# One full 32-bit matmul in place of three split ones, and a state update with high and low keys in one weight block

## What is computed

```python
# feed-forward branch (weights ternary, scales per output)
h = silu(x @ w1.T * s1) * (x @ w2.T * s2);  h = gelu(h @ h1.T * sh1);  h = gelu(h @ h2.T * sh2);  y = h @ w3.T * s3
# attention branch: gated linear attention over chunks of 64 tokens
b = cumsum(gt)                                   # log decay per key
o = (qt * exp(b)) @ S + A @ vt                   # A[i,j] = sum_k q[i,k] k[j,k] exp(b[i,k]-b[j,k]), j <= i
S = exp(btot)[:, None] * S + (kt * exp(btot - b)).T @ vt
o = (o + shift * residual_weight) * silu(gate);  o = o * rms(o) * norm_weight;  y = o @ down_w.T
```

## Time and profile before

| | us |
|---|---|
| median of 3 runs | 1988.01 (1987.57 to 1988.39) |
| span of the profiled execution, first to last instruction | 1984.5 |
| TensorE matmuls busy | 1967.8 (99% of the span) |
| TensorE weight loads busy | 1954.0 (98%) |
| VectorE busy | 1576.1 (79%) |
| ScalarE busy | 1258.2 (63%) |
| GpSimd busy | 68.6 (3%) |

### The profile page before, as it was taken

The page is one execution under the profiler, slowest core; times in us unless marked ns, Lnnn a source line. Parts: engine busy times, 40 slices in busy tenths (PEclk is TensorE's granted clock), DMA queues, the critical chain, the costliest instruction groups (busy, mean ns, idle before and its releaser), DMA issues.

```text
span 1984.5 us, 46801 instructions
## 1 busy us (share of the span) xinstructions
PE 1967.8 (99%) x17508; PEld 1954.0 (98%) x17508; DVE 1576.1 (79%) x4242; ACT 1258.2 (63%) x2495; POOL 68.6 (3%) x104
## 2 busy tenths in 40 slices
PE   7999999999999999999999999999999999999998
PEld 7999999999999999999999999999999999999998
DVE  7787778877788887787877788777888777878777
ACT  5665656666566666566656566665667665666565
POOL 0000000000000000000000000000000000000000
PEclk9999999999999999999999999999999999999999
DMA  8000000000000000000000000000000000000000
GB/s 302 7 12 12 12 7 6 12 12 12 12 1 12 12 12 12 12 1 12 12 12 12 7 6 12 12 12 12 1 12 12 12 12 12 1 12 12 12 7 7
DMA packets 23360, 34.22 MB, mean 17 GB/s; under 512 B 2945, under 2 KB 19713, under 8 KB 23186
## 3 DMA queue, kind: packets, MB, share of 16 engines
q1 hardware_dynamic: 23186, 31.46, 4.7%
HBM read 23.07 MB, written 8.39 MB: 16 GB/s over the span
## 4 chain that ended last, share of the span: by engine, by line
PE 94%; issue 2%; DVE 2%; ACT 1%; SPq 1%; DMA 0%; POOLq 0%; POOL 0%; DVEq 0%; ACTq 0%
PE fb L363 62%; PE ab L363 24%; PE ab L567 2%; PE ab L508 1%; PE ab L433 1%; PE ab L497 1%; PE fb L648 1%; PE ab L560 0%; SPq L271 0%; PE ab L559 0%; DVE hid0l L937 0%; DMA small<-stage_w 0%; ACT raw L801 0%; PE ab L558 0%; SPq L276 0%
## 5 line engine op out<-in xcount | busy, mean ns | idle before, releaser
L363 PE MATMUL fb<-hid1h,wwhole 128*128 128x256 f32 x2048 | 473.7, 279 | 0.2 <-DVE hid1l L854 0.2
L363 PE MATMUL fb<-hid1l,wwhole 128*128 128x256 f32 x2048 | 468.6, 276 | 0.0
L363 PE MATMUL fb<-hid0l,wwhole 128*128 128x256 f32 x2048 | 465.9, 276 | 0.0
L363 PE MATMUL fb<-hid0h,wwhole 128*128 128x256 f32 x2048 | 465.8, 276 | 0.0
L363 PEld LDWEIGHTS fb<-hid1h,wwhole 128*128 128x128 f32 x2048 | 384.7, 188 | 2.6 <-issue 0.4
L363 PEld LDWEIGHTS fb<-hid1l,wwhole 128*128 128x128 f32 x2048 | 384.7, 188 | 0.0
L363 PEld LDWEIGHTS fb<-hid0h,wwhole 128*128 128x128 f32 x2048 | 384.5, 188 | 0.0
L363 PEld LDWEIGHTS fb<-hid0l,wwhole 128*128 128x128 f32 x2048 | 384.4, 188 | 0.0
L801 ACT ACTIVATE raw<-fb,sh_s 128x256 f32<-128x256 f32 x512 | 213.0, 467 | 111.5 <-PE fb L363 110.6
L363 PE MATMUL fb<-xntl,wwhole 128*128 128x256 f32 x1024 | 237.5, 276 | 0.0
L363 PE MATMUL fb<-xnth,wwhole 128*128 128x256 f32 x1024 | 237.5, 276 | 0.0
(11 more groups left out here) (210 smaller groups left out, 4597.7 us busy)
## 6 DMA issues: line engine op xcount, KB each, us to landing
xin<-x SPq DMA_DIRECT2D x32, 256.0 KB, 2.7
out<-xin SPq DMA_DIRECT2D x32, 256.0 KB, 2.2
stage_more<-stage_w SPq DMA_DIRECT2D x6, 512.0 KB, 7.4
sgate<-stage_w SPq DMA_DIRECT2D x4, 512.0 KB, 4.7
shift<-stage_w SPq DMA_DIRECT2D x4, 512.0 KB, 5.2
v<-stage_w SPq DMA_DIRECT2D x4, 512.0 KB, 5.6
raw<-stage_w SPq DMA_DIRECT2D x3, 512.0 KB, 6.3
mixed<-stage_w SPq DMA_DIRECT2D x3, 512.0 KB, 8.6
```

The costliest lines, as they stand in the source:

```text
L363: mm = pe.matmul(o, a, b, start=start and i == 0, stop=stop and i == len(pairs) - 1)
```

## The change

Chunk 1's product with its own scores becomes one full 32-bit matmul `v[:, 1] x att[:, 1]` per block `d`; `atth`/`attl` keep two blocks, and in half 1 only chunk 0 of `v` is split. The decayed keys' high and low parts lie side by side in one 128-wide weight block (`kd`), so one matmul against `vh` gives the high keys' product on partitions 0 to 63 and the low keys' on 64 to 127; the product of high keys and `vl` goes through a 64-wide weight block into partitions 0 to 63. The halves are added afterwards: ScalarE copies the upper half to SBUF, VectorE adds, and the split of the sum into `stateh`/`statel` (each written to both partition halves) is made at the end of half 0.

```diff
-        atth, attl = sb("atth", [P, 3, CH], F32R), sb("attl", [P, 3, CH], F32R)
+        atth, attl = sb("atth", [P, 2, CH], F32R), sb("attl", [P, 2, CH], F32R)
-        kdq = sb("kdq", [P, 2, N], F32R)
+        kdq = sb("kdq", [P, N], F32R)
+        kd, qhl = kdq[:].rearrange("p (c a k) -> p c a k", c=NC, a=2), kdq[:]
+        state_low, state = mixed[0:K, 0:DI], mixed[0:K, DI:2 * DI]
# TensorE, state_update
-                    for c in range(NC):
-                        hi, lo = (t[:, c, :, :].rearrange("p a k -> p (a k)") for t in (kdh, kdl))
-                        pairs += [(hi, vh[:, c, :]), (hi, vl[:, c, :]), (lo, vh[:, c, :])]
-                    wide(ab[3][:], pairs).then_inc(su_mm.sem, 1)
+                    hi_lo = [kd[:, c, :, :].rearrange("p a k -> p (a k)") for c in range(NC)]
+                    pe.matmul(ab[3][:], hi_lo[0], vh[:, 0, :], start=True, stop=False)
+                    for c in range(NC):
+                        pe.matmul(ab[3][rows(0), :], kd[:, c, 0, :], vl[:, c, :], start=False, stop=False)
+                    pe.matmul(ab[3][:], hi_lo[1], vh[:, 1, :], start=False, stop=True).then_inc(su_mm.sem, 1)
# TensorE, outputs
+                    pe.wait_ge(att_d.sem, att_d.at(me))
-                        mm = wide(o[:, CH:N], [(vh[:, 1, cols], atth[:, 2, :]), (vh[:, 1, cols], attl[:, 2, :]),
-                                               (vl[:, 1, cols], atth[:, 2, :])], start=False)
+                        mm = pe.matmul(o[:, CH:N], v[:, 1, cols], att[:, 1, :], start=False, stop=True)
# TensorE, before down in half 0
-                    pe.wait_ge(st_lo.sem, st_lo.at(seq))
+                    pe.wait_ge(st_sum.sem, st_sum.at(seq))
# ScalarE, silu(2) of half 1
+                    if m == 2 and p == 1:
+                        act.wait_ge(st_lo.sem, st_lo.at(seq))
# ScalarE, splits
-                act.activation(vh, v[:], ACT.Copy).then_inc(vhi_d.sem, 1)
+                used = NC if p == 0 else 1
+                act.activation(vh[:, 0:used, :], v[:, 0:used, :], ACT.Copy).then_inc(vhi_d.sem, 1)
-                        act.activation(kdh[:, c, :, :], ab[2][:, c * K:(c + 1) * K].unsqueeze(1).to_broadcast([P, 2, K]), ACT.Copy,
-                                       scale=rkn[:, c:c + 1]).then_inc(kd_hi.sem, 1)
+                        act.activation(kd[:, c, 0, :], ab[2][:, c * K:(c + 1) * K], ACT.Copy, scale=rkn[:, c:c + 1]).then_inc(kd_hi.sem, 1)
-                        act.activation(atth[:, 0:3:2, :], att[:], ACT.Copy).then_inc(att_hi.sem, 1)
+                        act.activation(atth[:, 0, :], att[:, 0, :], ACT.Copy).then_inc(att_hi.sem, 1)
-                        act.activation(stateh[:], ab[3][:], ACT.Copy).then_inc(st_hi.sem, 1)
+                        act.activation(state_low, ab[3][rows(1), :], ACT.Copy).then_inc(st_copy.sem, 1)
# ScalarE, last in half 0, behind the Square of line 836
+                    act.wait_ge(st_sum.sem, st_sum.at(seq))
+                    act.activation(stateh[rows(0), :], state, ACT.Copy)
+                    act.activation(stateh[rows(1), :], state, ACT.Copy).then_inc(st_hi.sem, 1)
# VectorE: low parts of v, kd, att cut in the same way; in place of line 1155
-                    dve.wait_ge(st_hi.sem, st_hi.at(seq))
-                    low(statel[:], ab[3][:], stateh[:]).then_inc(st_lo.sem, 1)
+                    dve.wait_ge(st_copy.sem, st_copy.at(seq))
+                    dve.tensor_tensor(state, ab[3][rows(0), :], state_low, ALU.add).then_inc(st_sum.sem, 1)
# VectorE, half 0, between lines 1168 and 1169
+                    dve.wait_ge(st_hi.sem, st_hi.at(seq))
+                    low(statel[rows(0), :], state, stateh[rows(0), :])
+                    low(statel[rows(1), :], state, stateh[rows(0), :]).then_inc(st_lo.sem, 1)
```

More of the change, by code:

```diff
@@ L169, in layer_program @@
         att = sb("att", [P, NC, CH])
-        atth, attl = sb("atth", [P, 3, CH], F32R), sb("attl", [P, 3, CH], F32R)
+        atth, attl = sb("atth", [P, 2, CH], F32R), sb("attl", [P, 2, CH], F32R)
         stateh, statel = sb("stateh", [P, DI], F32R), sb("statel", [P, DI], F32R)
-        kdq = sb("kdq", [P, 2, N], F32R)
-        kdh, kdl = (kdq[:, i, :].rearrange("p (c a k) -> p c a k", c=NC, a=2) for i in range(2))
-        qhl = kdq[:, 0, :]
+        kdq = sb("kdq", [P, N], F32R)
+        kd, qhl = kdq[:].rearrange("p (c a k) -> p c a k", c=NC, a=2), kdq[:]
+        state_low, state = mixed[0:K, 0:DI], mixed[0:K, DI:2 * DI]
         stats = sb("stats", [P, NC, 6])
@@ L207, in layer_program @@
         kd_hi, st_hi, q_hi = seq_sig("kd_hi", NC), seq_sig("st_hi", 1), seq_sig("q_hi", 1)
+        st_copy, st_sum = seq_sig("st_copy", 1), seq_sig("st_sum", 1)
         gelu1_d, hid1_hi, gelu2_d, hid2_hi = sig("gelu1_d", FB), sig("hid1_hi", 4), sig("gelu2_d", FB), sig("hid2_hi", 4)
@@ L575, in state_update @@
                     pe.wait_ge(cross_lo.sem, cross_lo.at(me))
-                    pairs = []
+                    hi_lo = [kd[:, c, :, :].rearrange("p a k -> p (a k)") for c in range(NC)]
+                    pe.matmul(ab[3][:], hi_lo[0], vh[:, 0, :], start=True, stop=False)
                     for c in range(NC):
-                        hi, lo = (t[:, c, :, :].rearrange("p a k -> p (a k)") for t in (kdh, kdl))
-                        pairs += [(hi, vh[:, c, :]), (hi, vl[:, c, :]), (lo, vh[:, c, :])]
-                    wide(ab[3][:], pairs).then_inc(su_mm.sem, 1)
+                        pe.matmul(ab[3][rows(0), :], kd[:, c, 0, :], vl[:, c, :], start=False, stop=False)
+                    pe.matmul(ab[3][:], hi_lo[1], vh[:, 1, :], start=False, stop=True).then_inc(su_mm.sem, 1)
                 def outputs():
@@ L594, in outputs @@
                         cols = slice(d * P, (d + 1) * P)
-                        first = [(vh[:, 0, cols], atth[:, 0:2, :]), (vh[:, 0, cols], attl[:, 0:2, :]), (vl[:, 0, cols], atth[:, 0:2, :])]
+                        first = [(vh[:, 0, cols], atth[:]), (vh[:, 0, cols], attl[:]), (vl[:, 0, cols], atth[:])]
                         if p == 1:
@@ L836, in half @@
                 act.activation(sq[:], sgate[:], ACT.Square).then_inc(sq_d.sem, 1)
+                if p == 0:
+                    act.wait_ge(st_sum.sem, st_sum.at(seq))
+                    act.activation(stateh[rows(0), :], state, ACT.Copy)
+                    act.activation(stateh[rows(1), :], state, ACT.Copy).then_inc(st_hi.sem, 1)
             act.wait_ge(prep_dve, len(CHUNKS))
@@ L1109, in half @@
                 dve.wait_ge(vhi_d.sem, vhi_d.at(me))
-                low(vl, v[:], vh).then_inc(vlo_d.sem, 1)
+                used = NC if p == 0 else 1
+                low(vl[:, 0:used, :], v[:, 0:used, :], vh[:, 0:used, :]).then_inc(vlo_d.sem, 1)
                 if p == 1:
@@ L1120, in half @@
                     for c in range(NC):
-                        dve.scalar_tensor_tensor(kdl[:, c, :, :], ab[2][:, c * K:(c + 1) * K].unsqueeze(1).to_broadcast([P, 2, K]),
-                                                 rkn[:, c:c + 1], kdh[:, c, :, :].bitcast(F32), ALU.mult, ALU.subtract).then_inc(kd_lo.sem, 1)
+                        dve.scalar_tensor_tensor(kd[:, c, 1, :], ab[2][:, c * K:(c + 1) * K], rkn[:, c:c + 1], kd[:, c, 0, :].bitcast(F32),
+                                                 ALU.mult, ALU.subtract).then_inc(kd_lo.sem, 1)
                 dve.wait_ge(mask_d.sem, mask_d.at(me))
@@ L1129, in half @@
                 dve.wait_ge(att_hi.sem, att_hi.at(me))
-                low(attl[:, 0:3:2, :], att[:], atth[:, 0:3:2, :]).then_inc(att_lo.sem, 1)
+                low(attl[:, 0, :], att[:, 0, :], atth[:, 0, :]).then_inc(att_lo.sem, 1)
                 if not (last and p == HALVES - 1):
```

## The result

The changed kernel takes 1966.97 us (median of 4 runs, 1966.12 to 1968.32) against 1987.95 for the kernel before: a ratio of 0.9895, 95% interval 0.9883 to 0.9907, or 21.0 us less. The forecast was 1966.3. Run again beside other kernels it gave 1967.55 against 1988.62, ratio 0.9895 (0.988 to 0.991).

What follows compares the result with a forecast made beforehand. TensorE was taken as the bound, its time being the number of matmul records times their pace. Outputs 14.3 plus state update 7.4 gave 21.7 us off 1988.0, so 1966.3 us, 1.1% faster; range 1963.3 to 1972.6.

Steps and rivals of the forecast that it cites:

- The bound: TensorE in the steady loop: waits for nobody, matmuls busy 1967.8 of 1984.5 us; time is records times pace.
- The outputs: 128 blocks of outputs: two full 32-bit records replace three split ones, 0.112 us less each, 14.3 us in all.
- a block of 0.575: Sign in the profile after: blocks of the outputs repeat after 0.575 us instead of 0.69.
- rival E: Outputs: columns set the pace, each block loses 0.04, 5.1 us, against 7.4 gained for the state: 1985.7 us; chance 0.03.
- The passage between kinds: Each outputs block, going from split to full 32-bit matmuls and back at full height: no charge.
- rival D: Outputs: passing between split and full 32-bit costs 0.18 each way, 46.1 us over 128 blocks: 2012.4 us; chance 0.03.
- The state update: State update, once per sequence: six 512-column matmuls become four, 0.463 us less in each of 16, 7.4 us.
- Rival B: State update: passing into and out of 64-wide weights costs 0.36 each, losing 5.8 of the 7.4: 1972.1 us; chance 0.10.
- The cover: Edits off TensorE, priced at nothing: slack 0.96 us at the convolution, 0.65 at w3's last quarter; `msq` 0.46 later.
- Rival C: w3's last quarter, half 0: VectorE's chain does not move with TensorE, 4.2 us waited for, 1970.5 us; chance 0.10.
- The sum: Whole kernel: 14.3 + 7.4 = 21.7 us less, span 1962.8, median 1988.0 to 1966.3 us, 3.5 above the span.
- a record less is time less: TensorE throughout: each matmul record removed shortens the time, as long as the other engines keep up.

Runs made afterwards that it cites:

- the 48-wide block in all four matmuls: Changed kernel, gate factor's high and low weight parts in one 48-wide block, taken by all four matmuls that replace its six: 1969.08 us, ratio 0.9915.

## Why the prediction was right

**The bound.** Right. TensorE is paced by its records, and taking out 160 of them gave the time back at once, with VectorE and ScalarE doing more.

**The outputs.** Right in mechanism and size: 14.3 us forecast, 14.0 by the halves of the run with this part alone (0.43 and 0.45 a half). The two rules behind it were each tested: with 64 columns in place of 128 nothing changes, and a full 32-bit record takes 0.215 us for 256 columns, near the 0.232 of a `float32r` record of 512, as if it streamed its columns twice. By half of that, 0.108 us (an estimate), the two passes of 128 columns just fit under the weight load's 0.112, which is why four passes cost less than three here. The sign that the prediction named, a block of 0.575, came out at 0.59 and 0.57. The trace so bears out the four passes that the Trainium skill names in "FP8 and Floating Point Precision" (TensorE Precision Notes), and rival E, which counted them against three in columns, is refuted: the three never cost their columns. One reading on the way was not complete: the two records of line 560 stand 0.21 apart in the earlier trace rows and were called held up. The trace has matmuls of line 567, on 64 rows like it, between them:

```profile
83.08 0.37 PE L560 MATMUL ab<-small 64*128 64x128 f32 x1
83.08 0.43 PE L567 MATMUL ab<-work 64*128 64x64 f32 x2
83.29 0.27 PE L560 MATMUL ab<-small 64*128 64x128 f32 x1
```

The two lines run side by side, so the 0.21 doesn't show what a pair takes that has the engine to itself, and that it would be 0.11 was argued. For `v` and `att` the 0.11 is measured.

**The passage between kinds.** Right at nothing: outputs alone lost none of the 46 us of rival D. The first split matmul behind a full one lasts 0.36 in the profile, 0.08 more than the others, but it starts 0.08 early, 0.03 behind the full one's second record.

**The state update.** Right: 7.4 us forecast, 0.47 x 16 = 7.5. Rival B is refuted by the nearly equal time of the 64-wide and 128-wide blocks, 0.92 and 0.93 us for the four matmuls. The drain at a change of tiling mode, of which the Trainium skill warns in "TensorEngine Tiling (Array Packing)" (Key Properties), doesn't show for 64-wide weights on 128 rows: the two 64-wide matmuls and their neighbours go at the same 0.23. Whether the chip counts such weights as another mode, no run shows.

**The cover.** Right for the change itself: no new TensorE wait in the steady loop. `msq` starts 0.57 later in the half than before, not 0.46, mostly because the two low parts take 1.38 and not 1.2; the convolution still has 0.86 of idle ahead of it, where I had 0.96. But the list of who waits was incomplete: of the places named so far, the bank of the first gate product is the seam's tightest, not the convolution or the final sums. It cost nothing here and 0.2 to 0.3 us with 2.4 us more work. Rival C's place was sized well: 2.4 us more work there lost 0.96 where I had put 1.0. TensorE's waits account for 11.4 of these 16 us.

**The sum.** 21.7 us forecast, 21.3 by the steady halves ((0.906 + 0.428) x 16), 21.0 by the medians. Most of what is missing to 21.7 is the outputs' 0.3. I had carried 3.5 us between span and median from the kernel before; in the profiled run after, the time was 1966.91 for a span of 1965.0, 1.9 us. So not 3.5 but about 1.9 lies outside the span; the rest was a profiled execution quicker than the median. The forecast of the median didn't suffer from it, since it was taken from the median. The forecast of the span (1962.8) was 2.2 too low: 1.4 by the half behind the loop, 0.4 by what the steady halves fell short of 21.7, the rest by start-up and end.

What the prediction had no row for is the second pace. It took "a record less is time less" for a law. It held for this change, whose slow stretches lie where the kernel's before lie (1527 slow records against 1657, the difference almost all in the blocks of the outputs), and failed for the same idea on the gate factor. Since nothing in the prediction said that the stretches would stay, and an equally small edit (the 128-wide block for the low values) cost 10 us by moving them, that part of the hit was luck.

## What to carry to other kernels

Where TensorE is the bound, price a matmul by the larger of its weight load (0.112 us for a 128-wide block) and its columns, not by its columns: at 128 columns one full 32-bit matmul (two loads) beats three split ones, 0.22 us against 0.345, and at 256 it loses, 0.43 against 0.35. Put a split operand's high and low parts side by side in one weight block where it is at most 64 wide, and look for who else takes the bank that the later addition reads. Then compare the profile half by half: a saving of 0.2 us can be given back by a stretch that falls to another pace, and such a loss has no wait in any list.

## What was not expected of the hardware

- The same stream of matmuls with 128-wide weights and 256 columns runs at 113.3 or at 117.8 ns a record, at a full granted clock and with no wait. A stretch mostly keeps its pace until it is broken by transposes, 64-row, 81-row or full 32-bit matmuls, or by a single matmul that comes 0.05 us late with no wait in the list (37 us into halves of the run with the 48-wide block in all four matmuls): 126 or 122 records in 14 us of one execution. Over a kernel it came to between 7 and 20 us. In the kernel before and in the changed one it is the same in every sequence of the loop; in eight of the eleven other kernels it changes at least once from one sequence to the next. In the run with the state update alone the fast and the slow case part within a few ns behind the 81-row matmul. What chooses is open: the widths ahead, one more matmul, and VectorE's work elsewhere were each varied; with the first and the last the slow stretches moved, with the one matmul they didn't.
- The first half behind the hardware loop is 0.8 us longer than its sisters before the change and 2.2 after (2.1 in a second profiled execution, where I had expected it to vary by a microsecond or so). The surplus arises in one place: up to 34 us the half runs like its sisters to 0.01 us, 38 us into it the kernel before is 0.5 behind and the changed one 1.9, of which 1.1 is TensorE waiting for `hid1l`; the other 0.3 comes over the matmuls of h2 behind it, which go at the slow pace. The kernel with the 48-wide block in all four matmuls has no surplus there (59.39 us). Why `hid1l` is late is open.
- In several executions the first half of the first sequence is some 2 us longer, at a mean granted clock of 0.97 in that half (61.96 against 59.95 us in the run with the outputs alone, with 0.82 in the half's first 9.4 us and 1.00 behind); the profiled executions of before and after were spared.
